# A graph layer with a mixture of experts on one core: the last token block's messages in two column halves

## The reference

```
h   = layernorm(x)
x1  = x + relu(segment_sum(weight * (h @ W)[dst], src) + bias)
t   = layernorm(x1)
w, idx = top-2 of 64 of sigmoid(t @ Wg.T + bg), w normalised over the two
nx  = layernorm(t)
y   = sum over the two experts of w * ((silu(h1) * h3) @ W2 + b2),
      h1 = (nx * gamma + beta) @ W1 + b1,  h3 = (nx * gamma + beta) @ W3 + b3
z   = (silu(nxs @ Ws1 + bs1) * (nxs @ Ws3 + bs3)) @ Ws2 + bs2,  nxs = nx * gs + bs
out = x1 + y + z
```

## Time and profile before

| what | value |
|---|---|
| median of 3 runs | 431.43 us (430.48 to 431.75) |
| the profiled execution's own time | 432.0 us |
| its span in the trace | 430.2 us |
| mean granted TensorE clock | 0.983 |
| PE, DVE, POOL, ACT busy | 398.4, 213.2, 174.1, 156.9 us |
| weight loads on PE (PEld) | 207.4 us |
| DMA moved | 129.15 MB, mean 300 GB/s |

### The profile page before, as it was taken

The page is one execution under the profiler, slowest core; times in us unless marked ns, Lnnn a source line. Parts: engine busy times, 40 slices in busy tenths (PEclk is TensorE's granted clock), DMA queues, the critical chain, the costliest instruction groups (busy, mean ns, idle before and its releaser), DMA issues.

```text
span 430.2 us, 6405 instructions
## 1 busy us (share of the span) xinstructions
PE 398.4 (93%) x1898; PEld 207.4 (48%) x1899; DVE 213.2 (50%) x696; ACT 156.9 (36%) x387; POOL 174.1 (40%) x275
## 2 busy tenths in 40 slices
PE   6988999999999998999999999999898969897985
PEld 5656777756556557443443443443333433343331
DVE  8899998225666776633323323423313232123337
ACT  8767787322322220232332332332312321131232
POOL 2769996314655576523423323323312132121100
PEclk9999999999999998999999999999989998899999
DMA  7899971400002764499999999999999999999578
GB/s 254 211 335 408 406 287 47 137 31 26 25 25 63 281 232 146 151 402 410 400 407 405 410 406 407 406 407 406 405 406 409 405 408 404 406 399 406 231 273 325
DMA packets 44022, 129.15 MB, mean 300 GB/s; under 512 B 8054, under 2 KB 9270, under 8 KB 43858
## 3 DMA queue, kind: packets, MB, share of 16 engines
q1 hardware_dynamic: 38242, 120.45, 73.1%
q0 software_dynamic: 5744, 8.28, 5.4%
HBM read 119.64 MB, written 17.85 MB: 320 GB/s over the span
## 4 chain that ended last, share of the span: by engine, by line
PE 80%; issue 6%; DVE 5%; POOL 4%; DMA 3%; ACT 1%; SPq 1%; DVEq 0%; POOLq 0%; ACTq 0%
PE bank L1479 27%; PE bank L1342 13%; PE bank L1509 12%; PE bank L1501 5%; PE bank L1291 4%; PE bank L1467 4%; PE bank L1264 3%; DMA w<-totals 2%; PE bank L1236 2%; PE bank L1330 2%; PE bank L1363 2%; POOL M L502 1%; POOL AT L502 1%; PE bank L1351 1%; PE bank L1412 1%
## 5 line engine op out<-in xcount | busy, mean ns | idle before, releaser
L1136 DVE SCALAR_TENSOR_TENSOR osl<-bank,b13T,osl 128x64 f32<-128x64 f32 x128 | 27.5, 277 | 155.3 <-ACT osl L736 155.3
L1479 PE MATMUL bank<-w,xhT 128*64 128x512 f32 x368 | 87.6, 618 | 11.5 <-issue 11.5
L729 ACT COPY xh<-bank 128x512 f32<-128x512 f32 x33 | 19.4, 586 | 138.0 <-PE bank L1479 131.9
L1342 PE MATMUL bank<-HW,AT 128*128 128x512 f32 x128 | 58.2, 593 | 0.0
L1479 PEld LDWEIGHTS bank<-w,xhT 128*64 128x64 f32 x368 | 26.5, 141 | 56.5 <-issue 54.8
L596 POOL DMA_INDIRECT totals<-osl,A x16 | 16.4, 1028 | 80.2 <-PE bank L1467 72.1
L596 POOL DMA_INDIRECT totals<-GW,A x16 | 16.4, 1025 | 77.9 <-PE bank L1467 63.7
L1509 PE MATMUL bank<-w,osl 128*64 128x512 f32 x184 | 43.7, 593 | 1.6 <-DVE osl L1136 1.6
L592 POOL DMA_INDIRECT A<-nx_rows,A x33 | 34.3, 1039 | 12.3 <-issue 9.7
L1342 PEld LDWEIGHTS bank<-HW,AT 128*128 128x128 f32 x128 | 22.9, 191 | 21.0 <-issue 21.0
L645 ACT ACTIVATE osl<-iota,eT 128x128 f32<-128x128 f32 x90 | 27.8, 388 | 9.9 <-PE bank L1291 9.9
(11 more groups left out here) (238 smaller groups left out, 589.2 us busy)
## 6 DMA issues: line engine op xcount, KB each, us to landing
w<-in_L_ffn_W_dram SPq DMA_DIRECT2D x69, 1024.0 KB
A<-in_L_ffn_W_dram SPq DMA_DIRECT2D x15, 1024.0 KB
HW<-in_L_ffn_W_dram SPq DMA_DIRECT2D x8, 1024.0 KB
totals<-w SPq DMA_DIRECT2D x1, 4096.0 KB, 25.8
AT<-in_L_ffn_W_dram SPq DMA_DIRECT2D x4, 1024.0 KB
w<-totals SPq DMA_DIRECT2D x8, 512.0 KB, 7.4
out_dram<-X SPq DMA_DIRECT2D x8, 256.0 KB, 2.3
X<-in_x_dram SPq DMA_DIRECT2D x3, 512.0 KB, 9.5
```

What stands on the lines that cost most here:

```text
L1136: ins = v.scalar_tensor_tensor(hT[b][:, m, CAP * h:CAP * h + CAP], bank[4][:, (HC + m) * P + CAP * h:(HC + m) * P + CAP * h + CAP], b13T[: ...
L1342: ins = t.matmul(bank[4 + s % 2][:, :], AT[:, s % 2, k, :], HW[:, k, :], start=(k == 0), stop=(k == NB - 1))
L1479: ins = t.matmul(bank[2 + b][CAP * h:CAP * h + CAP, :], xe[b][:, c, CAP * h:CAP * h + CAP], up_w[v][:, h, :, c, :], start=(c == 0), stop=( ...
```

## The change

It has five parts.

1. **Two halves.** For the last block `sum_messages` makes 16 products of 128x256 instead of 8 of 128x512: first the left 256 columns, into bank 5, then the right ones, into bank 4. DVE's new `relu_add_halves` handles the left half on a semaphore of its own (`left_ps`), the right half on `out_ps`, with statistics of each half, joined by one `bn_aggr`.
2. **Bias from ACT.** ACT copies the bias into the two half banks beforehand (`fill_bias`), the products accumulate on it, and DVE needs one instruction for a half where `relu_add` has two for a block.
3. **One variance at a time.** For the last block `deviations` on POOL makes the first variance's inverse deviation and the negated mean before it turns to the second.
4. **The list's load** moves on SP from behind the seventh store of `nx_rows` to behind the sixth.
5. **Shared products.** Of four in front of `transpose_nx(7)` two stay; one goes behind the first `list_slots`, two behind the count, and `keep_busy` makes 14 transposes instead of 28.

```diff
@@ SP @@
-                if s == NB - 2:
+                if s == NB - 3:
                     for i in range(2):
                         sp.wait_ge(rec_out[i], 32 * ((DRAM_BLOCKS + 1 - i) // 2))
                     sp.dma_start(L, lists[:, :, 0:CAP * REC]).then_inc(list_in, 16)
+                if s == NB - 2:
                     sp.wait_ge(out_ps, NB)
@@ POOL, deviations @@
+                if last:
+                    link(g.tensor_scalar(ve[:, s, 0:1], mv1[:, s, 1:2], 1.0 + EPS, EPS * EPS, ALU.mult, ALU.add))
+                    link(g.tensor_tensor(rs[:, s, 0:1], ve[:, s, 0:1], mhalf[:, 0:1], ALU.pow))
...
                 g.tensor_scalar(nm[:, s:s + 1], mv1[:, s, 0:1], rs[:, s, 0:1], -1.0, ALU.mult, ALU.mult).then_inc(nm_ready, 1)
+                if last:
+                    link(g.tensor_scalar(ve[:, s, 1:2], mv1[:, s, 1:2], EPS, None, ALU.add))
+                    link(g.tensor_tensor(rs[:, s, 1:2], ve[:, s, 1:2], mhalf[:, 0:1], ALU.pow))
@@ ACT @@
+        message_halves = ((bank[4 + (NB - 1) % 2], slice(0, HALF)), (bank[4 + (NB - 2) % 2], slice(HALF, D)))
+            def fill_bias(half, s):
+                to, cols = message_halves[half]
+                act.wait_ge(x1_ready, s)
+                a.copy(to[:, cols], biasB[:, cols]).then_inc(bias_filled, 1)
...
+                if s == NB - 1:
+                    fill_bias(1, NB - 1)
                 if 1 <= s <= NB:
...
                     a.copy(nxT[t % 2].rearrange("p c n -> p (c n)"), bank[6][:, :]).then_inc(nxT_ready, 1)
+                if s == NB - 2:
+                    act.wait_ge(late_in, 64)
+                    fill_bias(0, NB - 2)
@@ DVE @@
+            def relu_add_halves(s):
+                for half, (messages, cols) in enumerate(message_halves):
+                    if half == 0:
+                        dve.wait_ge(left_ps, 1)
+                    else:
+                        dve.wait_ge(out_ps, s + 1)
+                    ins = v.scalar_tensor_tensor(X[:, s, cols], messages[:, cols], 0.0, X[:, s, cols], ALU.max, ALU.add)
+                    if half == 0:
+                        need(mark(ins))
+                    else:
+                        ins.then_inc(x1_ready, 1)
+                        dve.wait_ge(x1_ready, s + 1)
+                    c_st = mark(v.bn_stats(st12[:, 6 * half:6 * half + 6], X[:, s, cols]))
+                need(c_st)
+                v.bn_aggr(mv1[:, s, :], st12).then_inc(mv1_ready, 1)
@@ PE, sum_messages @@
+                if s == NB - 1:
+                    for n in range(2 * ks[0], 2 * ks[-1] + 2):
+                        half, k = n // NB, n % NB
+                        messages, cols = message_halves[half]
+                        if k == 0:
+                            pe.wait_ge(bias_filled, half + 1)
+                        ins = t.matmul(messages[:, cols], AT[:, s % 2, k, :], HW[:, k, cols], start=False, stop=(k == NB - 1),
+                                       skip_group_check=True)
+                        if n == NB - 1:
+                            ins.then_inc(left_ps, 1)
@@ PE, the end @@
-                if b == 2:
+                if b == 1:
                     pe.wait_ge(x1_ready, NB)
-            for b in range(4):
+            for b in range(2):
                 shared(b)
             transpose_nx(NB - 1)
...
-            shared(4)
+            shared(2)
             rank(NB - 1)
...
+            shared(3)
+            shared(4)
...
-            keep_busy(bank[0], 28)
+            keep_busy(bank[0], 14)
```

More of the change, by code:

```diff
@@ L221, in moe_gnn @@
         st6 = small[:, 142:148]
+        st12 = small[:, 168:180]
         share = small[:, 224:224 + 2 * NB].rearrange("p (s k) -> p s k", k=2)
@@ L267, in moe_gnn @@
         out_ps = sem("out_ps")
+        left_ps, bias_filled = sem("left_ps"), sem("bias_filled")
+        HALF = D // 2
+        message_halves = ((bank[4 + (NB - 1) % 2], slice(0, HALF)), (bank[4 + (NB - 2) % 2], slice(HALF, D)))
         x1_ready = sem("x1_ready")
@@ L546, in deviations @@
                 pool.wait_ge(mv1_ready, s + 1)
-                g.tensor_scalar(ve[:, s, 0:1], mv1[:, s, 1:2], 1.0 + EPS, EPS * EPS, ALU.mult, ALU.add)
-                link(g.tensor_scalar(ve[:, s, 1:2], mv1[:, s, 1:2], EPS, None, ALU.add))
-                link(g.tensor_tensor(rs[:, s, :], ve[:, s, :], mhalf[:, :], ALU.pow))
+                last = s == NB - 1
+                if last:
+                    link(g.tensor_scalar(ve[:, s, 0:1], mv1[:, s, 1:2], 1.0 + EPS, EPS * EPS, ALU.mult, ALU.add))
+                    link(g.tensor_tensor(rs[:, s, 0:1], ve[:, s, 0:1], mhalf[:, 0:1], ALU.pow))
+                else:
+                    g.tensor_scalar(ve[:, s, 0:1], mv1[:, s, 1:2], 1.0 + EPS, EPS * EPS, ALU.mult, ALU.add)
+                    link(g.tensor_scalar(ve[:, s, 1:2], mv1[:, s, 1:2], EPS, None, ALU.add))
+                    link(g.tensor_tensor(rs[:, s, :], ve[:, s, :], mhalf[:, :], ALU.pow))
                 g.tensor_scalar(nm[:, s:s + 1], mv1[:, s, 0:1], rs[:, s, 0:1], -1.0, ALU.mult, ALU.mult).then_inc(nm_ready, 1)
+                if last:
+                    link(g.tensor_scalar(ve[:, s, 1:2], mv1[:, s, 1:2], EPS, None, ALU.add))
+                    link(g.tensor_tensor(rs[:, s, 1:2], ve[:, s, 1:2], mhalf[:, 0:1], ALU.pow))
                 link(g.tensor_tensor(ratio[:, s:s + 1], ve[:, s, 0:1], rs[:, s, 0:1], ALU.mult))
@@ L1056, in _ @@
             for s in range(1, NB + 2):
-                if s <= NB:
+                if s < NB:
                     relu_add(s - 1)
+                elif s == NB:
+                    relu_add_halves(s - 1)
                 if s == 1:
@@ L1338, in sum_messages @@
                         pe.wait_ge(x1_ready, s - 1)
+                if s == NB - 1:
[8 more added lines that the diff above has]
+                            ins.then_inc(left_ps, 1)
+                    if ks[-1] == NB - 1:
+                        ins.then_inc(out_ps, 1)
+                    return
                 for k in ks:
```

## The result

The changed kernel took 433.12 us (median of 20 runs, 430.82 to 437.91), the kernel before 431.51 us in the same comparison (20 runs, 430.48 to 433.26). The ratio is 1.0036, with a 95% interval of 1.0019 to 1.0054: slower, where 430.6 us was forecast, with no difference as the likeliest outcome (0.60), and above the range's upper end of 432.3. (The ratios of this document leave out a run that lies more than 1.5% above the fastest of its kernel, 437.91 here and 436.49 in one experiment, and they are not quotients of the medians.)

A forecast was written before the change was run, and what follows sets the result against it. The expert weights' DMA stream was taken as the bound. Messages 0, plus 1.15, minus 0.15, minus 0.2 gave 0.8 us: 432.0 to 431.2, forecast 430.6 because the median lies 0.57 lower; range 429.2 to 432.3.

The forecast's parts named there:

- What bounds the kernel: Expert stage, from about 180 us: the weights' DMA stream bounds; its end is its start (load at 177.91) plus its bytes.
- Messages, DVE, ACT: Last block: messages gain 0; DVE behind them 1.27 us less (0.7 to 1.3); ACT's bias copies lie in idle time.
- The rival of the half-width pace: PE's messages: 256-column records take 0.43 us like whole ones, everything behind moves 6.9 us, 437.5 us; chance 0.05.
- POOL and the list's load: Block 5's scatters: earlier list load ends POOL's 0.81 us wait; POOL starts on the variance 0.7 us earlier.
- One variance at a time: POOL before block 7's normalisation: chain of 1.26 us instead of 1.74, 0.45 less (0.3 to 0.5).
- The second variance: POOL before `stacked(6)`: its add and power take 0.95 us more there, losing 0.15 of the 1.15 us gained.
- Shared products: Before block 7's transposes: moving two frees PE at 157.2; left, they cost 0.6 us. Longer work behind the count costs 0.2.
- The clock: Half clock, 166.8 to 170.2, at the idle transposes: if it stays, end 0.6 us earlier; if it moves, 0.85; 0.8 taken.
- the gain is eaten: POOL's scatters don't move up, or slow clock hits block 7's routing and list; 0.2 us stay, 431.2; chance 0.17.

The follow-up runs named there:

- the one with the gap alone: Kernel before, order unchanged, shared products of blocks 2 and 3 cut to 32 of 512 columns to open the gap before block 7's transposes: 434.02 us, ratio 1.0051.
- parts 1 to 4: Changed kernel with the shared products and 28 idle transposes put back as in the kernel before: 430.62 us, ratio 1.0000.
- five other kernels with these parts: Changed kernel with one or both PE gaps filled, or blocks 3 and 4 cut; part 5 undone plus unread products, or last store earlier: 1.0025, 1.0026, 1.0047, 1.0009, 0.9996.
- the same with the products: Kernel before with two unread 97x128x512 products and 14 transposes replacing the 28 transposes behind the count: 431.81 us, ratio 1.0002.
- the changed kernel with its front gap filled: Changed kernel plus 12 idle transposes on PE in front of block 7's transposes: 432.64 us, ratio 1.0025.
- the one with blocks 3 and 4 cut: Changed kernel with 28 transposes back behind the count and shared products of blocks 3 and 4 cut to 32 of 512 columns: 433.89 us, ratio 1.0047.
- part 5 with the gap filled: Kernel before with only the shared products moved, plus 18 idle transposes in front of block 7's transposes: 432.24 us, ratio 1.0006.

## Why the prediction was wrong

**What bounds the kernel** held. The span less the stream's start is 252.3 us before and 251.2 to 252.8 in all others but the one with the gap alone (254.7): the end moves with the first load.

**Messages, DVE, ACT** held. 0.22 us a record for 0.215; 0.42, 0.43 and 0.21 us on DVE for 0.42, 0.42 and 0.19; the copies of the bias took 0.38 and 0.37 us for 0.4. The rival of the half-width pace is out.

**POOL and the list's load** failed in its reason and by half in size. "Before, it waited 0.81 us for the list": it did not. The profile names the releaser that came last by its record, and here the named DMA had nothing to do with the gap. POOL came to the variance 0.35 us earlier and not 0.7, of which 0.21 are the shorter second scatter. Nor was the load itself as early as forecast: SP stood in front of it for block 4's scatters, which "have long landed", until 150.60, and it went out 1.1 us earlier against `HW` than before, not 2. One variance at a time gave the rest of the normalisation's 0.76 us: 0.41 for a forecast of 0.45. (The forecast's own terms, 1.74 - 0.36 - 0.13 + 0.07, make 1.32 us and a gain of 0.42, not 1.26 and 0.45.) The second variance cost nearly nothing in parts 1 to 4 (0.75 us gained at the transposes, 0.72 at the list) for a forecast of 0.15. But in five other kernels with these parts only 0.09 to 0.17 us were left at the list, for the two long DVE instructions above, a delay that no term of the sum has.

**Shared products** is the step that made the result wrong. "Two of them are out of the way now ... so PE is free at 157.2, ahead of 158.3. Left as they were they would have cost 0.6 us." Left as they were they cost 0.00: POOL had gained only half, and the four products just fit. And the sentence held the cause without a price: PE free at 157.2, work at 158.3. I had put down a gap of 1.1 us where one of 0.54 had been, called it idle time, and counted it as nothing. It became 1.65 us, and it took the granted clock from full to half for 13.7 us.

**The clock.** "If the slow stretch stays where it is in time" or "moves with the work", and "the lull in PE's work moves too": all cases treated the slow stretch of the earlier trace rows as a thing of fixed length that shifts. The rival "the gain is eaten" had the right place, "the slow clock falls on block 7's routing and the list", but was priced at the gain of 0.6 us and no more. From the rows it could have been priced: block 7's work from the transposes to the list, 7.2 us from 159.45 to 166.63, is mostly PE's and doubles in part; it measured 9.9 us from 159.28 to 169.18, 2.7 more.

The Trainium skill bears on this: "TensorE: Matmul & The Clock Gate", Part 1, section "HAM oscillation — how this bites in real kernels", describes a PE that waits for data, is throttled, and starts the next work cold. The trace agrees in this order of events, but its waits, the 1.65 and 2.40 us above, are shorter than those that the section tells of. The prediction cited the same page only for where the fall lies, and did not ask what a new gap does.

## What to carry to other kernels

Work on PE that looks free to move may be what keeps its clock up: before moving it, write down the gap that it leaves and price the work behind that gap at half rate. If the gap has to be, try to fill it with transposes that nobody reads: 2 us of them were worth about 4 where the gap was 2.40 us, and nothing that could be told in the changed kernel, where it was 1.65. And don't take a releaser's name for the cause of a wait: first look at a kernel in which the alleged cause stands elsewhere, and see whether the gap changes.

## What the runs showed of the hardware

The clock does not come back as soon as PE is busy. In the change PE was busy all of 162.5 to 167.5, at half rate, and most of the rest up to 174, but for 0.9 us in front of the list. Where the clock fell in the lull in front of the list, it stayed at half for 6.8 us with two products of 97x128x512 behind it, and for 3.4 us with transposes in their place: before against the same with the products, and the changed kernel with its front gap filled against the one with blocks 3 and 4 cut. Each was seen in one profiled execution, and in part 5 with the gap filled, which has the same products, it did not fall at all.

A store of 256 KB that is queued behind 3 MB on the same queue landed 5.6 to 9.0 us after its issue, against 2.0 to 2.3 for its like with nothing large in front. In the kernel before, the last one landed at 165.4, 1.4 us ahead of the list's end at 166.9; in parts 1 to 4 it landed last, and 0.4 of the 0.7 us gained at the list were lost there.

POOL stood 0.81 us in front of block 5's first scatter in all 13 kernels, whether the profile named a DMA or a DVE instruction as the releaser, and 0.17 to 0.44 us in front of block 6's.

Two DVE instructions on 128x2 and 128x32 elements took 1.14 and 1.03 us instead of 0.22 and 0.17 in five kernels, each time ending with an instruction of POOL beside them.
